# Scales spread in two fp32r rounds, chunk 0's state ahead of its scores, nine output matmuls ahead of the last product, and head coefficients copied behind the raw values

## The reference

```python
# attention branch, 32 heads of 128, 8 key/value groups, chunks of 128 tokens
q, k = rope(xn @ Wq.T), rope(xn @ Wk.T);  v = xn @ Wv.T
dt = softplus(xn @ Win.T + dt_bias);      g = dt * -exp(A_log_bias)
G = cumsum(g) within a chunk
y_intra = ((q k^T) * causal exp(G_i - G_j)) @ (v * dt)
state   = state * exp(G_last) + (k * exp(G_last - G))^T (v * dt)   # per chunk
y_inter = (q * exp(G)) @ state of the chunks before
y = y_intra + y_inter
y = y / sqrt(mean(y^2 over 128) + 1e-5) * gnorm_w
y = y * silu(xn @ Wg.T)
out = y @ Wo.T
# second branch: 16 experts, 2 picked per token, and a shared expert
```

## Time and profile before

| | |
|---|---|
| median of 3 runs | 2130.53 us (2129.3 to 2133.38) |
| profiled execution | 2131.05 us |
| its span, first to last instruction | 2129.2 us |
| mean granted TensorE clock | 0.98 |
| busy: PE, DVE, ACT, POOL | 2009.1, 1630.6, 1117.0, 879.7 us |

### The profile page before, as it was taken

The page is one execution under the profiler, slowest core; times in us unless marked ns, Lnnn a source line. Parts: engine busy times, 40 slices in busy tenths (PEclk is TensorE's granted clock), DMA queues, the critical chain, the costliest instruction groups (busy, mean ns, idle before and its releaser), DMA issues.

```text
span 2129.2 us, 31978 instructions
## 1 busy us (share of the span) xinstructions
PE 2009.1 (94%) x9216; PEld 1508.5 (71%) x9216; DVE 1630.6 (77%) x2905; ACT 1117.0 (52%) x2347; POOL 879.7 (41%) x705
## 2 busy tenths in 40 slices
PE   5799999999999999999899999999999999988992
PEld 3577777777777777767677777777777777777881
DVE  5887777777777777757877777777777777747996
ACT  5455555555555555452455555554555455537881
POOL 2243433434343434343254444343434444434661
PEclk9999999999999999999999999999999999999996
DMA  6322121212121212135121212121212121228778
GB/s 252 101 58 54 47 60 49 59 44 64 38 68 37 69 39 69 39 88 180 50 70 40 70 39 66 38 69 35 69 39 69 39 69 38 61 85 274 230 230 325
DMA packets 147515, 182.05 MB, mean 86 GB/s; under 512 B 12935, under 2 KB 89319, under 8 KB 147454
## 3 DMA queue, kind: packets, MB, share of 16 engines
q1 hardware_dynamic: 137310, 155.52, 25.2%
q0 software_dynamic: 8704, 25.21, 3.3%
q10 hardware_dynamic: 1440, 0.58, 0.1%
HBM read 152.90 MB, written 28.37 MB: 85 GB/s over the span
## 4 chain that ended last, share of the span: by engine, by line
PE 84%; DVE 8%; ACT 3%; DMA 2%; issue 2%; POOL 1%; SPq 0%; DVEq 0%; ACTq 0%; POOLq 0%
PE PJ L1223 14%; PE PJ L1225 14%; PE PJ L1224 13%; PE SC L1356 5%; PE OU L1223 5%; PE OU L1224 5%; PE OU L1225 5%; PE CS L1366 4%; PE YE L1377 3%; PE YI L1223 2%; DVE gm L1776 2%; PE OU L1319 2%; PE YI L1224 2%; PE YI L1225 2%; PE TR L1306 1%
## 5 line engine op out<-in xcount | busy, mean ns | idle before, releaser
L470 POOL TENSOR_TENSOR zl<-yb,zh 128x512 fp32r<-128x512 f32 x122 | 157.8, 1294 | 351.5 <-ACT zh L972 350.6
L756 POOL TENSOR_TENSOR gm<-gbc,amask 128x512 f32<-128x512 f32 x128 | 180.3, 1408 | 170.6 <-DVE wfl L1837 155.0
L1223 PE MATMUL OU<-woh,zh 128*128 128x512 f32 x488 | 226.6, 464 | 1.2 <-POOL zl L470 1.2
L1223 PE MATMUL PJ<-xnh,wqh 128*128 128x512 f32 x544 | 221.8, 408 | 4.5 <-DVE t L1765 2.7
L1223 PE MATMUL PJ<-xnh,wgh 128*128 128x512 f32 x512 | 221.1, 432 | 3.6 <-POOL wgl L726 3.6
L1225 PE MATMUL PJ<-xnh,wql 128*128 128x512 f32 x544 | 213.6, 393 | 0.0
L1224 PE MATMUL PJ<-xnl,wqh 128*128 128x512 f32 x544 | 213.5, 392 | 0.0
L972 ACT ACTIVATE zh<-yb 128x512 fp32r<-128x512 f32 x122 | 76.6, 628 | 250.3 <-PE OU L1225 181.3
L1225 PE MATMUL PJ<-xnh,wgl 128*128 128x512 f32 x512 | 203.4, 397 | 0.0
L1224 PE MATMUL PJ<-xnl,wgh 128*128 128x512 f32 x512 | 202.9, 396 | 0.0
L1868 DVE TENSOR_TENSOR yb<-YI,yb 128x512 f32<-128x512 f32 x96 | 66.4, 691 | 175.6 <-PE YI L1225 175.4
(11 more groups left out here) (551 smaller groups left out, 5338.6 us busy)
## 6 DMA issues: line engine op xcount, KB each, us to landing
gbc<-decay_exponents SPq DMA_DIRECT2D x128, 256.0 KB, 4.8
stage<-in_wq SPq DMA_DIRECT2D x72, 256.0 KB, 3.7
stage<-in_wg SPq DMA_DIRECT2D x64, 256.0 KB, 2.6
stage<-in_wo SPq DMA_DIRECT2D x64, 256.0 KB, 2.6
gbc<-in_wm SPq DMA_DIRECT2D x48, 256.0 KB
stage<-in_wkv SPq DMA_DIRECT2D x34, 256.0 KB, 2.6
experts<-in_wm SPq DMA_DIRECT2D x16, 512.0 KB, 5.6
experts<-expert_rows SPq DMA_DIRECT2D x16, 512.0 KB, 14.2
```

Of the source, the lines that this page charges most:

```text
L470: nc.gpsimd.tensor_tensor(lo[:], yb[:, c, :], hi[:].bitcast(F32), ALU.subtract).then_inc(S["zlo"], 1)
L756: g.tensor_tensor(gm[:, c % 2, :].rearrange("p (h i) -> p h i", h=HG), gbc[:, c % 2, :].rearrange("p (h i) -> p h i", h=HG), amask[:].unsq ...
L1223: nc.tensor.matmul(out_, a_hi, b_hi, start=first, stop=False)
```

## The change

It has four parts.

- The spread is made of two rounds of fp32r matmuls in place of one of fp32. ScalarE makes a high part `rmsh` of the scales behind the exponential, VectorE the remainder `rmsl` (`scales_low`); both lie in `ql`, which is free then. The first round starts the four banks with the high part, the second adds the low part.
- `chunk_state(0)` is issued ahead of the wait for the last rotation and of `scores(0)`.
- The last output product has nine matmuls ahead of `intra(3)` and three behind it.
- On VectorE `head_coefs` moves from the start of a step behind `v_rows`, `scales_low` follows it, and the product with the gate of chunk 0 moves from the end of the step to the last chunk, ahead of `yt`.

```diff
+        rmsh, rmsl = ql[:, 0, :], ql[:, 1, :]
...
-            rsln=1, rms=1, zhi=4,
+            rsln=1, rms=1, rmshi=1, zhi=4,
...
-            vlo=1, gmask=4, zlo=4,
+            vlo=1, gmask=4, zlo=4, rmslo=1,
...
                 a.activation(zhf[:], zhf[:], ACT.Exp, scale=-0.5).then_inc(S["rms"], 1)
+                at.before("spread", 1)
+                at.wait("rms", 1)
+                a.activation(rmsh, zhf[:], ACT.Copy).then_inc(S["rmshi"], 1)
 
             def z_hi(at, c, hi=zh):
                 at.wait("z", c + 1)
                 if c == 0:
+                    at.wait("rmslo", 1)
...
             def spread_scales(at):
-                at.wait("rms", 1)
+                at.wait("rmslo", 1)
...
-                for c in range(NCH):
-                    cs = slice(c * SUMS, (c + 1) * SUMS)
-                    ins = nc.tensor.matmul(TOU[c][:], pick[cs, :], zhf[cs, :], start=True, stop=True)
+                for part in (rmsh, rmsl):
+                    for c in range(NCH):
+                        cs = slice(c * SUMS, (c + 1) * SUMS)
+                        ins = nc.tensor.matmul(TOU[c][:], pick[cs, :].bitcast(F32R), part[cs, :], start=part is rmsh,
+                                               stop=part is rmsl)
...
                         proj_g(0)
                         if first and half == 0:
                             turn_decays(1)
+                        chunk_state(0)
                         at.wait("rope", 5)
                         scores(0)
                         for c in range(NCH):
-                            if c < 3:
+                            if 0 < c < 3:
                                 chunk_state(c)
...
                             elif c == 2:
-                                out_proj(at, 3, range(HG // 2))
+                                out_proj(at, 3, range(HG - 1))
                         if not first:
-                            out_proj(at, 3, range(HG // 2, HG))
+                            out_proj(at, 3, range(HG - 1, HG))
...
+            def scales_low(at):
+                at.wait("rmshi", 1)
+                v.tensor_tensor(rmsl, zhf[:], plain(rmsh), ALU.subtract).then_inc(S["rmslo"], 1)
...
+                        def gate_rows(c):
+                            at.wait("ysq", c + 1)
+                            if c == 0:
+                                at.wait("gated", 4)
+                            yv = yb[:, c, :].rearrange("p (h i) -> p h i", h=HG)
+                            v.tensor_tensor(yv, yv, gate[:, :, c * P:(c + 1) * P], ALU.mult).then_inc(S["u"], 1)
...
-                            head_coefs()
                             rope(0, 0)
                             v_rows()
+                            head_coefs()
                             if first:
                                 route_ranks()
+                            if not first:
+                                scales_low(at)
                             rope(1, 0)
...
                             if c:
+                                if c == 3:
+                                    gate_rows(0)
                                 at.wait("yinter", c)
...
+                        gate_rows(1)
+                        gate_rows(2)
+                        if not first:
+                            late_acc(at, 3, 1 - b)
+                        elif half == 1:
+                            route_slots()
+                        gate_rows(3)
...
             def flush_z(half):
                 at = At(dve, half * STEPS + STEPS, half)
+                scales_low(at)
                 for c in range(NCH):
                     late_z(at, c)
```

More of the change, by code:

```diff
@@ L309, in build @@
             vraw=1, vhi=1, kn=1, dec=4, expg=3, vw=3, whi=4, tanh=4, ysq=4,
-            rsln=1, rms=1, zhi=4,
+            rsln=1, rms=1, rmshi=1, zhi=4,
             coef=1, roperd=5, rope=5, wsc=4, wlo=4, stt=3, yt=3, y=4, gated=4, u=4, z=4, accd=4,
-            vlo=1, gmask=4, zlo=4,
+            vlo=1, gmask=4, zlo=4, rmslo=1,
         )
-        LAGGED = {"ssq", "spread", "oproj", "rsln", "rms", "zhi", "z", "accd", "zlo"}
+        LAGGED = {"ssq", "spread", "oproj", "rsln", "rms", "rmshi", "rmslo", "zhi", "z", "accd", "zlo"}
         S = {k: sem("s_" + k) for k in per_step}
```

## The result

The changed kernel takes 2098.4 us (median of 4 runs, 2094.7 to 2102.49), the kernel before 2131.95 us in the same job (4 runs, 2129.3 to 2134.38): a ratio of 0.985, 95% interval 0.9833 to 0.9866. The forecast was 2098.0.

The account below looks back on a forecast made before the run. TensorE's instruction stream was taken to set the step. Gains 15.7 + 1.7 + 12.0 + 5.1 less 1.3 at the ends sum to 33.2 us; from 2131.05 this gives 2097.9, forecast 2098 us, range 2088 to 2116.

Parts of the forecast that it names:

- Nine matmuls ahead: Last output product: three more matmuls cover the 0.56 us stall ahead of the last product; 15.7 us in 28 steps.
- 2.3 us of tail removed: VectorE behind the last product: gating pass 0.69, coefficients 1.26 and 0.32 behind them leave the tail, while TensorE comes 0.56 earlier.
- Coefficients: VectorE's head coefficients behind the raw values: price between 0.18 us and 1.26 with 0.32 behind; the low one taken.
- The low end: Coefficients cost 0.18 us in their new place, GpSimd being idle there; the high end would lose 0.33 us a step.
- Waits for `roperd` between first and second steps: TensorE's waits for the rotation's third product, first to second step of each half: 0.8 and 0.9, together 1.7 us gained.
- Spread: Two fp32r rounds of 0.34 us each, four matmuls side by side: 0.40 us less a spread, 12.0 us in 30 steps.
- rival of serial rounds: The spread's eight matmuls run one after the other, 1.86 us a spread: 2138 us, slower; chance 0.06.
- State of chunk 0: Ahead of the scores of chunk 0, the state's two passes cover the wait for the last rotation: 0.17 us, 5.1 in 30 steps.
- Just enough: From scores to `intra(0)`: 3.65 us of remaining passes against a chain of 3.63 us; nothing counted as lost.
- Ends of the halves: Copy and subtraction unhidden +1.32 us, later last product +0.13, rounds save 0.80: net loss 0.65, 1.3 us for both halves.
- VectorE as the bound: Rival: VectorE or the scale chain becomes the bound, waits of 0.3 to 0.6 us a step, 2108 to 2116 us; chance 0.17.
- "0.2" of slack: Last query projection: its rotation is read 0.61 us before it starts; less the spread's 0.40, 0.2 us is left.

Follow-up runs that it names:

- first experiment: Kernel before with only the last output product cut nine and three: 2138.55 us, ratio 1.0051.
- fourth: Changed kernel with VectorE's order of before (coefficients ahead of the first rotation, gate product of chunk 0 at the step's end): 2127.06 us, ratio 0.9992.

## Why the prediction was right, step by step

The total held: 33.2 us by the sum, 32.9 by the spans. Its parts held unequally, and that the total came so near is in part luck: the steps gave 34.5 us where 32.8 were forecast (15.7 + 12.0 + 5.1), and 2.4 us of longer waits in the first two steps of the second half, which nobody had counted, took that back.

*Nine matmuls ahead.* The stall of 0.56 us went as worked out; the trace gives 0.61 a step, 17.1 us for 15.7. The prediction asked whether VectorE keeps up and answered with 2.3 us of tail removed against 0.56 us of earliness (0.70, counted from the last product, where the tail begins). That answer is what the whole gain of this part rests on: without it the part loses 9 us (first experiment) and the change 29 (fourth). What the prediction did not work out is the free time before, 0.16 us, with which it would have seen that the cut alone gains next to nothing, and that the coefficients' 1.58 us (1.26 + 0.32) suffice without the gating pass. That the cut alone loses follows from no such sum: the 0.10 us behind each wait was not known.

*Coefficients.* The low end, 0.18 us, was right, for the reason given: GpSimd is idle there. (The Trainium skill, SBUF, Who interferes with whom, has VectorE and GpSimd hold a shared pair of ports by turns; the rows agree in both places, 1.26 beside GpSimd's pair and 0.18 without it.)

*Waits for `roperd` between first and second steps.* 1.4 us of the 1.7.

*Spread.* Side by side, 0.34 and 0.33 us a round, together 0.67 us where 1.07 stood (medians by starts): 0.40 less, as forecast. The total was right, its split was not: the prediction put 0.11 us around each round, but one round alone takes 0.43 us and the second 0.24 more, so that 0.20 us stands once around the whole spread, as in fp32 (1.07 - 2 x 0.434). The rival of serial rounds is excluded, even for the order in which it seemed likeliest.

*State of chunk 0.* Here a step failed: "With the spread 0.40 us shorter, TensorE would be there 0.40 us sooner and wait 0.57". The last rotation's end was taken as fixed in time; it hangs on GpSimd's `zl`, which follows TensorE's own first output product. So the wait would have kept its 0.17 us. The move takes away that wait and the 0.10 us behind it, and some 0.11 is lost again at `intra(0)`, where the prediction had found "Just enough". The part is worth some 4 us (0.14 a step in the sum above, 0.13 when it is undone), not 5.1, and no cover of the spread's gain hangs on it. The error is small in the total only because the prediction had counted the 0.40 us once, under the spread.

*Ends of the halves.* From the last product to the first one behind the spread it is 14.99 us (909.12 to 924.11) where 14.75 stood (926.97 to 941.72), and the last product itself comes 0.11 later than the gain ahead of it would have it (0.48 us sooner at its start, 0.59 at `intra(0)`, medians): 0.35 us lost at each end; forecast 0.65. The spread's part shrank from 2.02 us (939.70 to 941.72) to 1.16, about as forecast; the exponential came 0.36 us sooner after the last product, which was not.

*VectorE as the bound.* This rival did not come true, but it is near: the prediction's "0.2" of slack at the last query projection is 0.21 us, and with one round fewer the next 0.24 us of gain were already lost there.

## What to carry to other kernels

When work is moved ahead of a stall on the bounding engine, it is taken from behind it: look for the engine that used it there as cover, and count that engine's free time at its next meeting point first. When a wait seems to grow because the waiter comes sooner, ask whether what it waits for is not itself released by the waiter. Test the parts of a change both ways, alone in the old kernel and undone in the new one; here the same cut is worth a loss of 9 us and a gain of 18.

## What the hardware showed that was not expected

- A wait of TensorE costs more than its length: the second product after it starts 0.33 to 0.34 us behind the first, where 0.23 is usual, so a wait of 0.09 us costs 0.19. At `intra(0)` of the changed kernel the first product starts on time, 0.06 us behind the end of `wfl`, and the second is late all the same (1268.74 and 1269.07). The longer interval is not peculiar to waits: it also stands behind the sums of squares (0.34) and behind the spread (0.34), where no wait is listed.
- Four matmuls of 32 rows take 0.43 us between their neighbours, a second four only 0.24 more; and the eight run as two groups of four whether they are queued part by part or chunk by chunk.
- VectorE's addition of two 128x512 fp32 tiles beside GpSimd's subtraction ended 0.55 us behind it in every steady step of every run here, whether it started 0.24 us behind the subtraction (1.60 us long, the kernel before) or 0.61 to 0.66 (1.22 us long in the changed kernel, 1.19 with the rounds alone). Without GpSimd it takes 0.69 (1259.66).
- Behind the 3.2 us wait for `st` in the first step of the second half the granted clock is 0.50, the lower of its two levels, for some 3 us (1004.40 to 1007.40, and the same in the second profile of the changed kernel); behind the 2.4 us of the kernel before it stays 1.00 (1019.70 to 1022.70). Passes of 512 columns start 0.43 us apart in that stretch, where 0.23 is usual.
